# Two graph layers on one core: clamps moved to GpSimd, the largest r spread by TensorE, six slots for adj, sums beside the tangents

## What is computed

```
h  = relu(layernorm(x))
mx = h @ weight.T;  h = tanh(|mx|/|h| * artanh(|h|)) * mx/|mx|          (mobius_matvec, proj)
h  = mobius_add(h, hyp_bias);  x_tangent = artanh(|h|) * h/|h|           (proj, logmap0)
support = adj @ x_tangent
xt = relu(logmap0(expmap0(support)));  x1 = x + expmap0(xt)              (with proj at each step)
h2 = relu(layernorm(x1))
l  = (context @ W_common.T) @ w_left + b_left;   r = the same with w_right, b_right
logits = leaky_relu(l[:, None] + r[None, :], 0.2), -inf where adj <= 0
out = x1 + relu(softmax(logits) @ h2)
```

## Time and profile before

| | us |
|---|---|
| median of three runs | 573.61 |
| lowest, highest | 572.56, 574.72 |
| profiled execution, its own time | 573.64 |
| its span in the trace | 571.8 |

### The profile page before, as it was taken

One profiled execution on the slowest core, in us unless ns is written; L12 is line 12 of the kernel. 1 busy time (PEld: TensorE's weight loads), 2 busy tenths in 40 slices (PEclk: granted clock), 3 DMA queues, 4 the chain that ended last, 5 costly groups with the idle time before them and its releaser, 6 DMA issues.

```text
span 571.8 us, 9585 instructions
## 1 busy us (share of the span) xinstructions
PE 488.3 (85%) x3207; PEld 419.0 (73%) x3207; DVE 463.6 (81%) x923; ACT 314.1 (55%) x466; POOL 267.7 (47%) x333
## 2 busy tenths in 40 slices
PE   1724879999699979999697648799999999999995
PEld 1623758888588858888586436688888888888884
DVE  4997877897889787898398999996969787878773
ACT  1675766786386847686386553535454535353521
POOL 6840006899969996877154998401011101020200
PEclk9975999999799997999899788999999999999998
DMA  7999899999799998999893010101111010101010
GB/s 165 201 230 226 198 226 233 281 285 324 221 268 305 292 311 199 299 284 300 221 286 91 21 37 1 38 20 38 22 36 29 29 32 25 39 18 38 1 38 18
DMA packets 91911, 84.75 MB, mean 148 GB/s; under 512 B 7600, under 2 KB 89776, under 8 KB 91872
## 3 DMA queue, kind: packets, MB, share of 16 engines
q1 hardware_dynamic: 54944, 47.60, 35.2%
q10 hardware_dynamic: 34512, 32.25, 20.1%
q0 software_dynamic: 2416, 4.41, 2.8%
HBM read 80.02 MB, written 4.21 MB: 147 GB/s over the span
## 4 chain that ended last, share of the span: by engine, by line
PE 56%; DVE 20%; DMA 8%; issue 5%; POOL 5%; ACT 4%; ACTq 1%; DVEq 0%; POOLq 0%
PE ps L734 34%; PE ps L705 21%; DVE room L985 5%; DMA room<-in_adj_dram 4%; DMA top_right<-h_room 2%; DVE room L1222 2%; ACT mask L856 2%; DVE room L1173 1%; DMA h_room<-top_right 1%; DVE room L1189 1%; POOL mask L490 1%; DVE mask L944 1%; POOL post L549 1%; DVE mask L997 1%; DVE room L1196 1%
## 5 line engine op out<-in xcount | busy, mean ns | idle before, releaser
L705 PE MATMUL ps<-room 128*128 128x256 f32 x1024 | 237.5, 393 | 38.1 <-DVE room L1103 23.0
L705 PEld LDWEIGHTS ps<-room 128*128 128x128 f32 x1024 | 200.3, 198 | 73.3 <-DVE room L985 37.2
L734 PE MATMUL ps<-room 128*128 128x258 f16 x2048 | 231.0, 276 | 21.7 <-POOL room L618 16.2
L734 PEld LDWEIGHTS ps<-room 128*128 128x128 fp8e4 x2048 | 200.0, 98 | 52.7 <-issue 16.9
L985 DVE STREAM_TRANSPOSE room<-room 128x512 f32<-128x512 f32 x256 | 172.1, 696 | 35.7 <-PE ps L705 16.8
L856 ACT ACTIVATE mask<-room,constants 128x1024 int8<-128x1024 f32 x128 | 146.2, 1145 | 85.5 <-DVE room L985 84.0
L632 POOL TENSOR_TENSOR h_room<-h_room 128x512 f32<-128x512 f32 x7 | 8.9, 1273 | 146.3 <-DVE post L1263 146.3
L1189 DVE SCALAR_TENSOR_TENSOR room<-mask,constants,room 128x512 int32<-128x512 int32 x64 | 61.2, 957 | 8.7 <-ACT room L906 8.7
L906 ACT ACTIVATE room<-relu_u,r_col 128x512 int8<-128x512 f32 x64 | 42.0, 713 | 41.1 <-PE ps L734 41.1
L481 POOL TENSOR_TENSOR mask<-mask,h_room 128x2048 f32<-128x2048 f32 x8 | 36.3, 4534 | 50.2 <-DVE room L1103 49.9
L906 ACT ACTIVATE room<-room,r_col 128x512 int8<-128x512 f32 x62 | 40.9, 712 | 32.9 <-PE ps L734 32.8
(11 more groups left out here) (158 smaller groups left out, 345.4 us busy)
## 6 DMA issues: line engine op xcount, KB each, us to landing
room<-in_adj_dram SPq DMA_DIRECT2D x136, 256.0 KB, 7.1
room<-in_adj_dram ACTq DMA_DIRECT2D x120, 256.0 KB, 7.8
mask<-in_L_gnn_context_dram SPq DMA_DIRECT2D x16, 256.0 KB, 11.8
xk<-in_x_dram POOLq DMA_DIRECT2D x32, 64.0 KB, 6.2
out_dram<-xk POOLq DMA_DIRECT2D x32, 64.0 KB, 5.4
h_room<-out_dram SPq DMA_DIRECT2D x32, 64.0 KB, 2.4
out_dram<-h_room SPq DMA_DIRECT2D x28, 64.0 KB, 1.7
mask<-in_x_dram SPq DMA_DIRECT2D x22, 64.0 KB, 4.3
```

The costliest lines, as they stand in the source:

```text
L705: mm = pe.matmul(acc[parity][:, h], xt[:, tangent_order.index(blocks_of(c, k)[j]), :], turned[:, k % TSLOTS, j * (CH // 2):(j + 1) * (CH / ...
L734: mm = pe.matmul(ps[:, 2 * t + w, 0:GW], part[slot(c, g)][:, kk, t * P:(t + 1) * P], G[w][:, k, :], start=(k == 0), stop=(k == NK - 1))
```

## The change

- The clamp of the squared norms to MIN_NORM2 and the addition of LN_EPS leave VectorE (lines 1126 and 1141) and go to GpSimd, at the head of `shrink` and in `affine`.
- The largest r: GpSimd widens the 128 numbers to 128 x 128, TensorE transposes them into PSUM behind block 0 of chunk 5, and VectorE reduces them from there after block 3 of chunk 5. The memory buffer and its two DMAs are gone. The first reduction is after block 15 of chunk 4. ScalarE's exponentials move from chunk 7 to chunk 6.
- Two more slots for tiles of adj lie in the last chunk's part of the mask, so chunks 0 to 6 turn six slots (`slot_of`) and the last chunk four. The array h, which lay elsewhere, takes that place until its norms are summed; SyncE waits for that (`roots_asked`) and then loads tiles 4 and 5 whole.
- GpSimd does eight steps of `beside` as soon as the tangents' scales and the context are there, instead of two after the last tangent; the steps that follow come in the same places of its stream.
- The bias parts `fb` lie in PSUM, one bank each.
- TensorE's loop over the chunks of the first layer is written out. In the second layer's room G[0] and the row of -left change places.

```
+BESIDE_FIRST = 8
...
-        loaded = view(room, o, [XSLOTS, RH, W], F32)
+        loaded = [view(room, o + n * RH * W * 4, [RH, W], F32) for n in range(XSLOTS)]
...
+        spare_loaded = [view(scratch, (NC - 1) * NK * CH + n * RH * W * 4, [RH, W], F32) for n in range(2)]
+        loaded += spare_loaded
+        tiles = (NC - 1) * NC
+        slot_of = [t % len(loaded) for t in range(tiles)]
+        slot_of += [n for n in slot_of[-len(loaded):] if n < XSLOTS] * 2
+        before = [max([u for u in range(t) if slot_of[u] == n], default=None) for t, n in enumerate(slot_of)]
...
+        fb = ps[:, 4:4 + XT_AHEAD, 0:D]
...
                 for g in range(NC):
-                    first_tiles = c == 0 and g < XSLOTS
-                    if not first_tiles:
-                        sp.wait_ge(block_turned, c * NK + L * (g - XSLOTS + 1))
-                    load_tile(sp, c, g, (0, 2, 1, 3) if first_tiles else LOW)
-                    if c == 0 and g == XSLOTS - 1:
+                    if c == 0 and g == XSLOTS:
                         load_context()
+                        sp.wait_ge(roots_asked, 1)
+                    t = c * NC + g
+                    if before[t] is not None:
+                        sp.wait_ge(block_turned, L * (before[t] + 1))
+                    load_tile(sp, c, g, LOW if t >= len(loaded) else (0, 2, 1, 3))
...
-            def store_largest():
+            def store_rows():
                 pool.wait_ge(neg_turned, 1)
                 for b in range(NQ):
                     pool.dma_start(nl_dram[:, b * Q:(b + 1) * Q], neg_rows[b * Q:(b + 1) * Q]).then_inc(nl_stored, 16)
+
+            def widen_largest():
                 pool.wait_ge(top_ready, 1)
-                pool.dma_start(top_dram, extreme[:, 0:1]).then_inc(top_stored, 16)
-
-            def everyones_largest():
-                pool.wait_ge(top_stored, 16)
-                pool.dma_start(top_row, top_dram.rearrange("p a -> a p").broadcast_to([P, P])).then_inc(top_loaded, 16)
+                nc.gpsimd.tensor_copy(top_wide, extreme[:, 0:1].broadcast_to([P, P])).then_inc(top_widened, 1)
...
+                chain(nc.gpsimd.tensor_scalar(post[:, 0:8], post[:, 0:8], MIN_NORM2, None, ALU.max))
                 chain(tt(post[:, 8:16], post[:, 0:8], powers[:], ALU.pow))
...
                 nc.gpsimd.tensor_scalar(post[:, 44:48], mv[:, :, 0], -1.0, None, ALU.mult)
+                chain(nc.gpsimd.tensor_scalar(post[:, 40:44], mv[:, :, 1], LN_EPS, None, ALU.add))
                 chain(tt(post[:, 48:52], post[:, 40:44], powers[:, 0:L], ALU.pow))
...
-            pool.wait_ge(xt_ready, NK)
-            beside(0)
-            beside(1)
+            pool.wait_ge(tangent_scales, 1)
+            for n in range(BESIDE_FIRST):
+                beside(n)
             for p in range(NC - 1):
                 shrink(p)
-                beside(3 * p + 2)
+                beside(BESIDE_FIRST + 3 * p + 0)
...
+                    if k == 0 and c == NC // 2 + 1:
+                        pe.wait_ge(top_widened, 1)
+                        pe.matmul(ps_top, top_wide, ident[:], start=True, stop=True).then_inc(top_spread, 1)
-            chunked(pe, product)
+            for c_ in range(NC):
+                product(c_, c_ % 2)
...
-                    chain(v.reduce_sum(post[:, 4:8], sq2, AX_X))
-                    v.tensor_scalar(post[:, 0:8], post[:, 0:8], MIN_NORM2, None, ALU.max).then_inc(sums_ready, 1)
+                    v.reduce_sum(post[:, 4:8], sq2, AX_X).then_inc(sums_ready, 1)
...
-                    chain(ins)
-                    v.tensor_scalar(post[:, 40:44], mv[:, :, 1], LN_EPS, None, ALU.add).then_inc(var_ready, 1)
+                    ins.then_inc(var_ready, 1)
...
-                    if c == NC - 2 and k == 15:
+                    if c == NC // 2 and k == 15:
                         dve.wait_ge(r_ready, 1)
                         v.reduce_max(extreme[:, 0:1], r_col[:], AX_X).then_inc(top_ready, 1)
                         dve.wait_ge(neg_ready, 1)
                         v.transpose(neg_rows, neg_l).then_inc(neg_turned, 1)
-                    if c == NC - 1 and k == 3:
-                        dve.wait_ge(top_loaded, 16)
-                        v.reduce_max(extreme[:, 1:2], top_row, AX_X).then_inc(top_ready, 1)
+                    if c == NC // 2 + 1 and k == 3:
+                        dve.wait_ge(top_spread, 1)
+                        v.reduce_max(extreme[:, 1:2], ps_top, AX_X).then_inc(top_ready, 1)
```

More of the change, by code:

```diff
@@ L149, in bass_two_graph_layers @@
         assert (NC - XSLOTS) % XSLOTS == 0
[L150 to L155, removed]
+        gw_bytes = NK * GW * 2
+        nl_even = view(room, nl_at + gw_bytes, [CH], F32)
+        G = [view(room, nl_at + w * (gw_bytes + CH * 4), [NK, GW], F16) for w in (0, 1)]
+        assert 2 * RH * W * 4 <= gw_bytes and gw_bytes + CH * 4 <= 3 * RH * W * 4
         slot_bytes = 2 * L * CH
@@ L181, in bass_two_graph_layers @@
         place = [NC * NK * CH]
+        spare_loaded = [view(scratch, (NC - 1) * NK * CH + n * RH * W * 4, [RH, W], F32) for n in range(2)]
[4 more added lines that the diff above has]
+        before = [max([u for u in range(t) if slot_of[u] == n], default=None) for t, n in enumerate(slot_of)]
+        behind = [min([u for u in range(t + 1, len(slot_of)) if slot_of[u] == n], default=None)
+                  for t, n in enumerate(slot_of)]
+        assert len(slot_of) == NC * NC and NK * CH == len(spare_loaded) * RH * W * 4
         def tmp(shape):
@@ L218, in bass_two_graph_layers @@
         v_rows, lr, extreme, neg_l = late([2, C]), late([2, NK]), late([2]), late([NK])
-        wlr, top_row, neg_rows = late([4]), late([P]), late([NK])
+        wlr, top_wide, neg_rows = late([4]), late([P]), late([NK])
         assert NK == Q
@@ L227, in bass_two_graph_layers @@
         ps_mx = [ps[:, n:n + 2, 0:2 * (D + 1)].rearrange("p n (a d) -> p n a d", a=2) for n in (2, 6)]
-        ps_v, ps_W = ps[:, 4, :], ps[:, 5, 0:P + 1]
+        fb = ps[:, 4:4 + XT_AHEAD, 0:D]
+        ps_v, ps_W, ps_top = ps[:, 4, :], ps[:, 5, 0:P + 1], ps[:, 4, 0:P]
         nl_dram = nc.dram_tensor("neg_left", (NK, P), F32, kind="Internal").ap()
-        top_dram = nc.dram_tensor("top_right", (P, 1), F32, kind="Internal").ap()
         weights_in, context_weights_in = sem("weights_in"), sem("context_weights_in")
@@ L236, in bass_two_graph_layers @@
         zeroed, ident_made, powers_made = sem("ident_zeroed"), sem("ident_made"), sem("powers_made")
-        adj_in = [sem(f"adj_loaded_{s}") for s in range(XSLOTS)]
+        adj_in = [sem(f"adj_loaded_{s}") for s in range(len(loaded))]
         block_turned, block_multiplied, half_signed = sem("block_turned"), sem("block_multiplied"), sem("half_signed")
@@ L254, in bass_two_graph_layers @@
         neg_ready, neg_turned = sem("neg_ready"), sem("neg_turned")
-        top_stored, top_loaded = sem("top_stored"), sem("top_loaded")
+        top_widened, top_spread = sem("top_widened"), sem("top_spread")
         exponents_ready, exponentials_done = sem("exponents_ready"), sem("exponentials_done")
@@ L285, in load_tile @@
         def load_tile(eng, c, tile, quarters):
+            n = slot_of[c * NC + tile]
             for b in quarters:
-                eng.dma_start(loaded[b * Q:(b + 1) * Q, tile % XSLOTS],
-                              adj_n[c, *run_and_half(c, tile), b]).then_inc(adj_in[tile % XSLOTS], 16)
+                eng.dma_start(loaded[n][b * Q:(b + 1) * Q], adj_n[c, *run_and_half(c, tile), b]).then_inc(adj_in[n], 16)
         def run_and_half(c, tile):
@@ L537, in beside @@
                 elif n == 2 * len(turns) + 1:
-                    store_largest()
+                    store_rows()
                 elif n == 2 * len(turns) + 2:
-                    everyones_largest()
+                    widen_largest()
                 elif n == 2 * len(turns) + 3:
@@ L557, in residual @@
                 pool.wait_ge(tanh_ready, p + 1)
-                chain = Steps(pool, post_step, p * POOL_POST + 3)
+                chain = Steps(pool, post_step, p * POOL_POST + 4)
                 chain(nc.gpsimd.tensor_scalar(TF, TH_, MAX_NORM, None, ALU.min))
@@ L567, in affine @@
                 pool.wait_ge(var_ready, p + 1)
-                chain = Steps(pool, post_step, p * POOL_POST + 6)
+                chain = Steps(pool, post_step, p * POOL_POST + 7)
                 nc.gpsimd.tensor_scalar(post[:, 44:48], mv[:, :, 0], -1.0, None, ALU.mult)
+                chain(nc.gpsimd.tensor_scalar(post[:, 40:44], mv[:, :, 1], LN_EPS, None, ALU.add))
                 chain(tt(post[:, 48:52], post[:, 40:44], powers[:, 0:L], ALU.pow))
                 tt(post[:, 36:40], post[:, 44:48], post[:, 48:52], ALU.mult).then_inc(norm2_ready, 1)
-            POOL_POST = 7
+            POOL_POST = 9
             def store_x1(p):
@@ L600, in _ @@
                 store_x1(p)
-                beside(3 * p + 3)
+                beside(BESIDE_FIRST + 3 * p + 1)
                 affine(p)
```

(13 more changed lines are left out.)

13 lines of the change are left out of this document (7 added, 6 removed).

## The result

The changed kernel takes 556.31 us (median of four runs, 554.63 to 557.25) against 573.09 us of the kernel before on the same chips; the ratio is 0.9713, with a 95% interval of 0.9659 to 0.9767. The forecast was 550, with a range of 544.5 to 559. So the direction and the range held; 16.8 us came where 23.5 were forecast, and the measured time lies just outside the forecast's own case (544.5 to 554) and inside that of the rival "late steps" (552 to 557). All times are medians of fast executions; a single slow one of 1310.12 us, of the version with both clamps back, is left out.

The account below looks back on a forecast made before the run. First-layer chunks can't beat TensorE's 28.1 us; 24.1 us there, lost to held clamps, slow clock and the largest r's transfers, less 2.1 plus 1.5 for the passage gives 23.5 off 573.6: 550 us, range 544.5 to 559.

Parts of the forecast that it names:

- the forecast's own case: Whole kernel: the forecast of 550 us holds, the time lands at 544.5 to 554 us; chance 0.62.
- late steps: GpSimd's eight steps, x1 at block 28 or the last chunk's four slots cost 1 to 3 us each: 552 to 557; chance 0.13.
- Part 1: First layer, both clamps to GpSimd: held clamps and the slow clock behind them go, 17.1 us gained.
- Part 2: Last chunks of the first layer, largest r through TensorE: memory transfers and the wait behind them go, 7.0 us gained.
- The rival that the rows of -left would leave a hole in chunk 4: Storing these rows in chunk 4 could leave a hole in the DMA rate: 0 to 4 us; no chance of its own.
- Part 3: Six slots of adj in chunks 1 to 6: cover 17.3 us instead of 10.4; earns nothing by itself.
- DMA-bound rival: First layer: the adj stream holds only 300 GB/s, a chunk takes 29.7 us, time 559 us; chance 0.13.
- Part 4: Chunk 0, eight GpSimd steps beside the tangents: they end at 101 us, shrink started at 101.34, so nothing is lost.
- Part 5: Tangents, bias parts in PSUM: VectorE's cost taken as 0, bounds +1.6 to -1 us for both engines.
- The slower rival, tangents held by the sums: Chunk 0: tangents wait for running GpSimd instructions, 20 us in all, time 570, or 582 at 2 us a pair; chance 0.07.
- Part 7: Passage behind the last chunk: the same two clamps go from VectorE, 1.5 us gained (0 to 3).
- the lost time moves on: Block 30: the next VectorE instruction stalls instead of the clamp, time 565 us; chance 0.05.

Follow-up runs that it names:

- the version with six and the later normed rows: Changed kernel with six steps of sums first, then two a chunk (three in chunk 4), ScalarE's normed rows one pair of blocks later: 551.15 us, ratio 0.9627.
- the version with seven: Changed kernel with seven steps of sums first, two in each of chunks 1 to 5, normed rows one pair of blocks later: 551.33 us, ratio 0.9618.

## Why the forecast was right, and where it was off

- **What bounds.** Right: TensorE's 28.1 us a chunk is the floor; two whole intervals of the changed kernel and four of the version with six and the later normed rows sit on it.
- **Part 1, the clamps.** The mechanism was right: a clamp that meets a product lasts as long as the product, in the earlier trace rows and again in the version with seven, and a chunk loses 6.0 to 7.4 us with it there. The size was not: 17.1 us forecast, 8.7 measured alone (2.5 us more were lost to the wait for the largest r in that run). The sum took each interval down to 28.1 us, as if nothing else stood just above. GpSimd's stream did, at 29.5 to 31.3 us, and in the changed kernel the intervals lose only 2.7 us when the clamps go back. What the clamps are worth is set by what else is late: about 3, 8.7 or 25.3 us.
- **Part 2, the largest r.** Right: 7.0 forecast, 7.5 measured alone, 7.1 when undone. VectorE waited 0.4 us for the transpose. The hole in the DMA rate was the store's. The rival that the rows of -left would leave a hole in chunk 4 fell: the fourth interval moved 300 GB/s. The Trainium skill's figure of 512 B for line rate (DMA: Bandwidth & Descriptors, Specifications) covers these rows of 128 B as well, yet only the single numbers did harm.
- **Part 3, six slots.** "Earns nothing by itself" was right; "without it part 1 would meet late landings" wasn't shown: with four slots the changed kernel takes the same time. The DMA-bound rival fell: 325 GB/s in the window from 210 to 238 us with TensorE never idle.
- **Part 4, the sums beside the tangents.** With part 1's size this is the step that failed. "They end at 101, shrink started at 101.34, so nothing is lost" held for that one date (they ended at 101.15, `shrink` started at 101.25), but its other side moved: VectorE's second sum of squares, for which `shrink` waits, now ended at 97.8 us, not at 101. And the period was not added up: shrink 3.7, sum 6.4, x1 3.0, store 2.6, product 4.6, affine 1.7, sum 6.4, load 2.4 are 31 us of one engine in a chunk that was to take 28.4; where a product takes the place of one of the two sums it is 29.5 us (101.25 to 130.73). The durations of the kernel before's own lines had shown it; its interval of 35.15 us with GpSimd busy for 32.52 was a hint, but the one before it had 21.04. Four intervals cost 8.2 us over 28.1 where 1.2 were left for them. Taking six first, two a chunk and opening the ring gave back 5.2 us (556.31 to 551.15; the ratios 0.9713 and 0.9627, their intervals just apart). What the eight early steps earned at all isn't known: no run has the changed kernel with two steps first.
- **Part 5, bias parts in PSUM.** Right, 0: the tangents' median is 346 ns against 352. The slower rival, tangents held by the sums, didn't come here, but it is real one step away: with both inputs in SBUF it cost 23.3 us. The 20 worked out for it are near, in part by luck: they had no term for TensorE's clock, which was granted at 0.67 to 0.92 in the five stretches of 10 us from 57 to 107 us. The Trainium skill's rule for one and for two inputs in SBUF (SBUF — State Buffer, Who interferes with whom) agrees with both runs.
- **Part 6, the loop.** 0 within 1 us: in the run with only the largest r, which has it too, the five intervals before the largest r are those of the kernel before, but for one that is 0.8 us longer.
- **Part 7, the passage.** 1.5 forecast, 0 measured: from TensorE's last block to its long run it takes 60.1 us before, 60.2 after and 60.0 with the clamps put back. Where the clamp waited 2.26 us the next instruction waits now. The clamp and the instruction behind it before, then that instruction in the changed kernel:

```profile
336.63 2.38 DVE L1141 TENSOR_SCALAR post<-mv 128x4 f32<-128x4 f32 x1
...
338.92 0.74 DVE L1189 SCALAR_TENSOR_TENSOR room<-mask,constants,room 128x512 int32<-128x512 int32 x1
```

```profile
317.64 3.02 DVE L1201 SCALAR_TENSOR_TENSOR room<-mask,constants,room 128x512 int32<-128x512 int32 x1
```

Line 1201 (1189 before) has two inputs in SBUF; before, clamp and wait and this instruction took the same 3.0 us together, 336.63 to 339.66. The rival "the lost time moves on" was wrong for the blocks and right here.

**By the terms**, in the profiled runs: chunk 0 ended 3.4 us earlier than taken (its first support turn at 89.4 instead of the 92.8 of the earlier trace rows; 0.2 of it is the difference between two views of the same turn; the low clock ended 3 us sooner and the dip at 84 us was gone), which I had left in the range only; the six intervals took 6.4 us more than forecast, the passage 1.5 more. -3.4 + 6.4 + 1.5 = 4.5 us, the same as the span's distance, 552.8, from the forecast's 548.3. The median of the runs is 1.7 us above the profiled one. The first term is luck: nothing in the change aims at it, and the versions with six and seven steps first ended chunk 0 anywhere from 90.0 to 92.5 us. Without it the profiled execution's distance from the forecast would be 7.9 us, some 558 us and near the range's upper end.

**The whole.** The two parts that were to bring the first layer's gain brought 8.7 and 7.5 us alone, 16.2 of the 16.8 measured together. That the time lies in the range is the rival "late steps", to which 0.13 was given, not the forecast's own case with 0.62. Of the signs named beforehand these failed: four of six intervals are outside 28.1 to 28.6 us, and the layer ends at 291.8 us, not by 290.

## What to carry to other kernels

Before a stall is taken out of a period, add up what each engine has to do in that period and what the longest ring of waits is, and let the gain end at the highest of these, not at the best engine's floor; here GpSimd's own steps came to 29.5 and 31.4 us by turns, over TensorE's 28.1, and a ring through three engines to 28.9. A small VectorE instruction that GpSimd can hold ends only when the GpSimd instruction beside it does (the clamp, 4.55 us beside 4.51), so it pays to keep it from being held (the tangents by one operand in PSUM, the clamps by another engine), but the gain shows only where nothing else is as late. When a part is undone to price it, the answer holds for that version only: the clamps cost about 3 us where GpSimd was the bound and 25.3 where it wasn't.

## What the runs showed of the hardware

- 128 numbers of 4 bytes, stored from 128 partitions, took 12.6 and 11.9 us to land, and for 6 to 7 us behind them all queues together moved 94 and 104 GB/s instead of 343 and 333. The prediction had held this possible; the run with the largest r by memory shows that it is the store and not chance.
- A tangent with one input in SBUF, a column scalar in SBUF and one input in PSUM was not held in any of 32 instances, most of them beside GpSimd's products and sums (306 to 349 ns); with both inputs in SBUF one took 4378 ns beside a product of 4.50 us.
- A wait for GpSimd can pass to the next instruction that can be held: with the clamp gone from the passage the two-input instruction behind it took the whole wait, 3.02 us for it alone against 3.03 for both before.
- A full busy column isn't a floor: TensorE's was full in intervals of 28.6 us and in intervals of 28.1 us with the same blocks.
